# First head's scores before the last query tile, the last value block's cast on ScalarE, and a new order of transposes, in a cross-attention and expert kernel

## The reference

```
x = x + xattn(layernorm(x), ctx)     # 16 heads of 32 columns
x = x + ffn(layernorm(x))            # 8 experts, gated by a narrow zone of a sigmoid

xattn:  q = (x @ Wq + bq) / sqrt(32);  k, v = split(ctx @ Wkv + bkv)
        q, k rounded to 127 steps per row and head; v to 127 steps per column
        attn = softmax(q k^T) per head, rounded to 255 steps per row
        out  = (attn @ v) @ Wp + bp
ffn:    weights = gate(sigmoid(x @ Wr / temperature))
        out = sum_e weights_e * (silu(x @ Wg_e) * (x @ Wu_e)) @ Wd_e
```

## Time and profile before

| | |
|---|---|
| median of 3 runs | 743.71 us (742.88, 743.71, 746.09) |
| profiled execution | 742.73 us, of which the span of the trace is 740.9 us |
| TensorE busy | 623.8 us, 84% |
| VectorE busy | 573.1 us, 77% |
| ScalarE busy | 461.5 us, 62% |
| GpSimd busy | 371.5 us, 50% |
| DMA queue of SP | 114.48 MB, 71.5% of 16 engines |
| span of attention on VectorE | 133.08 to 445.5 us |

### The profile page before, as it was taken

The page is one execution under the profiler, slowest core; times in us unless marked ns, Lnnn a source line. Parts: engine busy times, 40 slices in busy tenths (PEclk is TensorE's granted clock), DMA queues, the critical chain, the costliest instruction groups (busy, mean ns, idle before and its releaser), DMA issues. The chain is left out here.

```text
span 740.9 us, 15739 instructions
## 1 busy us (share of the span) xinstructions
PE 623.8 (84%) x5298; PEld 325.9 (44%) x5298; DVE 573.1 (77%) x974; ACT 461.5 (62%) x552; POOL 371.5 (50%) x394
## 2 busy tenths in 40 slices
PE   6999999566777777777767687799999999999993
PEld 2444443233434343343434355455555555555551
DVE  4997778999999999999999996784746537455330
ACT  6334358688899999999999997243434435344321
POOL 5254457544666675757576754215334453343503
PEclk9999999999999999999999999899999999999997
DMA  7767767999999999999999995459895887977804
GB/s 246 195 150 168 167 142 124 189 170 179 181 171 191 211 174 213 174 217 181 206 180 210 188 201 107 133 178 183 223 250 127 235 220 184 254 137 213 149 6 57
DMA packets 325908, 131.25 MB, mean 177 GB/s; under 512 B 300901, under 2 KB 300901, under 8 KB 325865
## 3 DMA queue, kind: packets, MB, share of 16 engines
q1 hardware_dynamic: 318688, 114.48, 71.5%
q0 software_dynamic: 7168, 16.26, 10.6%
q10 hardware_dynamic: 8, 0.01, 0.0%
HBM read 44.33 MB, written 12.06 MB: 76 GB/s over the span
## 5 line engine op out<-in xcount | busy, mean ns | idle before, releaser
L946 ACT ACTIVATE work<-spare,exp_bias 128x2048 int16<-128x2048 f32 (+1 forms) x128 | 255.5, 1996 | 32.0 <-DVE exp_bias L1276 30.4
L1267 DVE TENSOR_SCALAR_CACHE_REDUCE spare<-psum,q_step_now 128x1024 f32<-128x1024 f32 x128 | 162.2, 1274 | 0.1
L632 POOL CAST work<-work 128x2048 int16<-128x2048 uint8 x63 | 119.1, 1890 | 81.8 <-DMA work<-work 67.5
L1258 DVE TENSOR_SCALAR_CACHE_REDUCE spare<-psum,q_step_now 128x2048 f32<-128x2048 f32 x64 | 150.4, 2350 | 0.1
L1679 PE MATMUL psum<-keys_region,work 128*128 128x512 f16 x256 | 73.1, 383 | 52.1 <-DVE spare L1267 28.9
L1679 PE MATMUL psum<-keys_region,bias_hl 128*128 128x512 f16 x256 | 71.9, 382 | 32.1 <-DVE spare L1267 28.3
L737 POOL DMA_INDIRECT work<-x_rows,slot_tok x32 | 50.1, 1564 | 97.1 <-DVE slot_w L1453 73.8
L749 POOL DMA_INDIRECT out_dram<-keys_region,slot_tok x32 | 51.7, 1617 | 74.1 <-ACT keys_region L1025 67.1
L1521 PE MATMUL psum<-work,spare 128*128 128x480 f16 (+1 forms) x396 | 79.2, 360 | 0.9 <-DVE work L1426 0.9
L1521 PE MATMUL psum<-work,keys_region 128*128 128x480 f16 x384 | 78.9, 366 | 0.0
L1639 PEld LDWEIGHTS psum<-values_region,work 128*128 128x128 f16 x2048 | 67.4, 96 | 24.2 <-DMA work<-work 12.5
(11 more groups left out here) (222 smaller groups left out, 1014.0 us busy)
## 6 DMA issues: line engine op xcount, KB each, us to landing
spare<-in_L_ffn_Wd_dram SPq DMA_DIRECT2D x8, 1024.0 KB, 15.6
spare<-in_L_ffn_Wg_dram SPq DMA_DIRECT2D x7, 1024.0 KB, 5.7
spare<-in_L_ffn_Wu_dram SPq DMA_DIRECT2D x7, 1024.0 KB, 12.1
work<-in_ctx_dram SPq DMA_DIRECT2D x3, 1024.0 KB, 5.7
work<-work SPq DMA_TRANSPOSE x181, 3.6
token_region<-in_L_xattn_Wkv_dram SPq DMA_DIRECT2D x2, 1024.0 KB, 6.9
resid<-in_x_dram SPq DMA_DIRECT2D x2, 1024.0 KB, 8.7
x_rows<-work SPq DMA_DIRECT2D x8, 256.0 KB, 2.3
```

The costliest lines, as they stand in the source:

```text
L632: nc.gpsimd.tensor_copy(p_T_int[h % 4 // 2], pair_bytes[h % 4 // 2]).then_inc(unpacked, 1)
L946: nc.scalar.activation(last_int[h % 2] if words and h >= H - 2 else p_int[h % 4], scores, ACT.Exp, bias=exp_bias[:, h % 4:h % 4 + 1], scal ...
L1258: nc.vector.tensor_scalar(staged[h % 4], psum[:, at:at + 4, :].rearrange("p b k -> p (b k)"), q_step_now[:, h:h + 1], None, ALU.mult, ALU.min,
L1267: nc.vector.tensor_scalar(staged[h % 4][:, 1024 * c:1024 * c + 1024], psum[:, at:at + 2, :].rearrange("p b k -> p (b k)"), q_step_now[:, h ...
```

## The change

It has five parts.

1. TensorE makes the scores of head 0 of the first tile after query tile 6, and query tile 7 after them. VectorE stages head 0 and gives its bias first, and takes query tile 7 then.
2. The cast of the last value block goes from VectorE to ScalarE, behind `cut_queries(2)`. `cut_queries(3)` goes behind the first exponential.
3. The steps in `q_step_now` come from ScalarE for the first tile as well, straight from `q_quantum` with the factor in the instruction; the tensor `q_step` is gone, and so are VectorE's two instructions for steps.
4. On SP the transpose of the last value block goes from before p_0 to before p_1, and the two of the last pair of query tiles from before p_0 to behind p_3 and p_4. `vT_in` becomes two semaphores.
5. GpSimd waits for all transposed queries behind its first three unpacks and not ahead of clearing the second half of `q_now`.

```diff
@@ SP
-            for i in range(2):
-                transpose_values(2 * i)
-                transpose_values(2 * i + 1)
-                transpose_queries(i + 2)
-            sp.wait_ge(vT_in, 16 * DK)
+            transpose_values(0)
+            transpose_values(1)
+            transpose_queries(2)
+            transpose_values(2)
...
                     sp.wait_ge(exp_done, u + 1)
                     passed()
+                    if first and h == 1:
+                        transpose_values(DK - 1)
+                    if first and h % 2 and h < 4:
+                        sp.wait_ge(vT_in[h // 2], 32)
...
+                    if first and h in (3, 4):
+                        transpose_queries(DK - 1, range(h - 3, h - 2))
@@ POOL
-            for b in range(2):
-                pool.wait_ge(qT_in[b], 16 * QT // 2)
             pool.wait_ge(q_full, QT)
             pool.wait_ge(wp_ready, DK)
             clear_queries(own, 1)
             queries_now(0, 1)
             norm_base = own.base + own.n
+            pool.wait_ge(vT_in[0], 32)
             unpack(0, 0, True)
+            pool.wait_ge(vT_in[1], 32)
             unpack(0, 2, True)
             unpack(0, 4)
             pool.wait_ge(unpacked, 3)
+            for b in range(2):
+                pool.wait_ge(qT_in[b], 16 * QT // 2)
             next_queries(1, 0)
@@ ACT
             cut_queries(2)
-            cut_queries(3)
+            act.wait_ge(v_rounded, DK)
+            nc.scalar.activation(v_T_int[:, DK - 1, :], v_i16[:, DK - 1, :], ACT.Copy).then_inc(last_halved, 1)
...
-                nc.scalar.activation(q_step_now[:, these], q_step[:, bass.ds(i, 1), these].rearrange("p a h -> p (a h)"), ACT.Copy
-                                     ).then_inc(steps_ready, 1)
+                nc.scalar.activation(q_step_now[:, these], q_quantum[:, bass.ds(i, 1), these].rearrange("p a h -> p (a h)"), ACT.Copy,
+                                     scale=-1.0 / WS).then_inc(steps_ready, 1)
...
+            for n in range(2):
+                copy_steps(0, n)
+
             def attention_tile(i, first, after_rows, following=True):
                 for h in range(H):
                     u = H * i + h
+                    if first and h == 1:
+                        cut_queries(DK - 1)
@@ DVE
             query_tiles(2, 4, 2)
-            halve_values(3)
             query_tiles(3, 6, 1)
-            nc.vector.tensor_scalar(q_step_now[:, :], q_quantum[:, 0, :], -1.0 / WS, None, ALU.mult).then_inc(first_steps, 1)
-            query_tiles(4, 7, 1)
-            own = Steps(dve, dve_step, head + query_steps * (DK + 1))
-            own.link(nc.vector.tensor_scalar(q_step[:, :, :], q_quantum[:, :, :], -1.0 / WS, None, ALU.mult))
...
                     stage_whole(i, h, first)
-                    if h:
+                    if first and h == 0:
+                        make_bias(i, h)
+                        query_tiles(DK, QT - 1, 1)
+                    elif h:
                         make_bias(i, h - 1)
...
-            dve.wait_ge(first_steps, 1)
+            dve.wait_ge(steps_ready, 2)
@@ PE
-            for t in range(QT):
+            def queries(t):
...
+            for t in range(QT - 1):
+                queries(t)
...
                 if first and h == 1 and n == 0:
-                    pe.wait_ge(q_out, DK + 1)
+                    pe.wait_ge(q_out, DK)
...
                 for n in range(2):
                     scores(i, 0, n, first)
+                if first:
+                    queries(QT - 1)
                 for h in range(0, H, 2):
                     scores(i, h + 1, 0, first)
+                    if first and h == 6:
+                        pe.wait_ge(q_out, DK + 1)
```

## The result

| | before | changed |
|---|---|---|
| median of 20 runs | 743.36 us (741.91 to 746.09) | 744.89 us (743.03 to 747.71) |
| ratio of the runs | | 1.0022, 95% interval 1.0012 to 1.0031 |
| profiled execution, its span | 742.73, 740.9 | 745.16, 743.4 |

The changed kernel is slower by 1.53 us in the medians and by 0.22% in the ratio. The forecast was +0.35 us, no change that a measurement can tell; 0.22% is inside 0.5% and inside the stated range, but the interval excludes 1, and the size is more than four times the forecast.

What follows compares the result with a forecast made beforehand. The prediction took VectorE to bound attention, with the DMA engines near their limit: -0.95 us at the start and +1.3 of stalls make +0.35, so 743.71 becomes 744.1 us, with 742.0 to 746.4 for 8 in 10.

Steps and rivals of the forecast that it cites:

- The bound and the gap: Attention: VectorE, busy 239.89 of 240 us, sets the time; behind p_0 the DMA engines stand idle some 5 us.
- The start: Start of attention: VectorE 0.95 us earlier from head 1 on.
- The 3.16 us: VectorE's start: the cast of the last value block 1.53, first steps 0.64 and all steps 0.99 us go.
- The new wait for ScalarE: Behind query tile 6, VectorE waits for head 0's steps from ScalarE, 127.88 to 129.85: 2.0 us.
- The stalls: From head 1 on, transposes displaced among the probabilities land late and cost VectorE 1.3 us.
- p_1, forecast 1.4 late and 0.1: Transpose p_1 lands at 148.6 where TensorE wants it at 147.2: 1.4 us late, costs 0.1.
- p_3, forecast 0.4 late and no cost: Transpose p_3, issued at 148.1, lands at 152.55: 0.4 us late, which costs nothing.
- the server with fixed times: SP's transposes, served in order: 1.85 us from issue, then 1.35 for 8 blocks or 2.6 for 16.
- the cover of 1.3: Values on TensorE: a probability transpose can be 1.3 us late before VectorE has to wait.
- p_5, forecast 2.2 late and 0.9: Transpose p_5 lands at 159.2 where 156.9 is wanted: 2.2 us late, 0.1 already lost, costs 0.9.
- p_7, forecast 0.3: Transpose p_7, behind a load of weights, lands at 164.4 where 162.8 is wanted: costs 0.3 us.
- The rival in which the queue doesn't recover: From p_5 on SP's queue stays full and p_7 to p_13 miss too: up to +4.4 us, 748.1; chance 0.12.

Runs made afterwards that it cites:

- e5: The kernel before, run again without an edit: attention 320.78 us against 320.68, ratio 0.9993.
- e1: Changed kernel with the last value block's transpose moved ahead of p_0 and the last query pair's directly behind p_0: attention 319.86 us, ratio to the kernel before 1.0002.
- e4: Kernel before with only the new order of SP's transposes and GpSimd's waits: attention 322.23 us, ratio to the kernel before 1.0036.
- e9: The changed kernel again, without further edits: attention 323.24 us, ratio to the kernel before 1.0030.
- e10: e1 again, without further edits: attention 320.20 us, ratio to the kernel before 0.9992.
- e2: Changed kernel with only the last value block's transpose moved ahead of p_0: attention 321.19 us, ratio to the kernel before 1.0017.
- e3: Changed kernel with only the last query pair's two transposes moved to behind p_0: attention 321.97 us, ratio to the kernel before 1.0007.
- e8: Changed kernel with six more throwaway matmuls ahead of the values in four slots of the first tile: attention 322.99 us, ratio to the kernel before 1.0036.
- e11: e7 again, without further edits: attention 319.26 us, ratio to the kernel before 0.9966.
- e6: Changed kernel with ScalarE's two copies of steps ahead of its cut of query tiles 4 and 5: attention 321.54 us, ratio to the kernel before 1.0003.
- e7: Changed kernel with the edits of both e1 and e6: attention 319.84 us, ratio to the kernel before 0.9969.

## Why the prediction was right in its main mechanism and short in size

**The number.** 744.1 against 744.89 looks closer than it was. The 743.71 that it started from was the median of three runs; of twenty it is 743.36, so that the difference, +0.35 against +1.53, is the fair comparison. The prediction also named a sign of being wrong in the main, a shift of attention by more than 1.5 us. From the mark the shift was 1.90 us (1.07 in the times of the two profiles as they stand, which don't start alike), so by this sign the prediction was wrong. So the main mechanism held, the sizes did not, and the lower clock was missing; the terms below say where.

**The bound and the gap: right.** VectorE had no idle before (0.56 us at 199 us in e5), and every idle that came is in the time. SP's gap behind p_0, the late p_1, p_3 and p_5, and TensorE's waits at values(1) and values(5) came as described.

**The start, forecast -0.95: too large.** It was -0.65 in the first pair of profiles. The prediction had the first staging 5.01 us behind the mark (129.85 - 124.84), then 2.53 for head 0 with its bias, then 2.04 for query tile 7. Measured were 4.93, 2.47 and 2.47, which makes 9.87. So the step that failed is that tile 7 costs the same wherever it stands: its small instruction at 132.12 took 0.60 us, where it took 0.17 in the kernel before and in e1. In e1 tile 7 took 2.04, and head 1 came at 9.38.

The gain at the start is in any case hardly larger than its scatter. The old order had head 1 at 10.52, 10.18 (e5) and 9.86 (e4), mean 10.19; the order of the change at 9.38 to 10.28 in seven profiles (changed, e9, e1, e10, e2, e3, e8), mean 9.77. That is 0.4 us on average, and -0.04 in the pair of e9 and e5.

A part of this scatter is in small instructions that wait for GpSimd. The 3.16 us read off as removed work held such waits too. The first steps ran 129.41 to 130.14 before, 0.73 us for 16 columns; a subtraction on GpSimd ended at 130.10. In e5 the ends were 129.04 and 129.00, and all steps ended 0.09 behind the next subtraction, at 131.86 and 131.77. In e4 the first steps took 0.38. In e11 the same kind of small instruction ran 1.14, and GpSimd's subtraction beside it ended with it:

```profile
130.39 1.14 DVE L1195 TENSOR_SCALAR scratch<-row_scales 128x16 f32<-128x16 f32 x1
```

```profile
130.34 1.15 POOL L684 TENSOR_TENSOR work<-spare,work 128x512 f16<-128x512 f32 x1
```

131.53 and 131.49. In the changed kernel's timeline of VectorE, at 125.41 and 132.12, 1.10 and 0.60 us stand at the two places, where 0.17 was the time of the same instruction in tile 7 of e5. The first ended at 126.51, a subtraction at 126.48. The second ended at 132.72 with no subtraction beside it (GpSimd had begun a multiplication at 132.01), and what held it isn't shown. So a hold can go on to the next small instruction when its bearer is removed, and isn't saved then. It depends on how the streams fall against each other: in e2 and e8 both instructions took 0.17 to 0.19. (The first hold in the changed kernel lay under the wait for ScalarE; the second did not.)

**The new wait for ScalarE, forecast 2.0: right.** It was 1.31 behind a tile that was itself 0.93 late, 2.2 together, and 2.01 in e1.

**The stalls, forecast 1.3: they were 1.83, and 1.82 in e9.** In the changed kernel, by terms:

- p_1, forecast 1.4 late and 0.1: TensorE waited 1.29, VectorE lost nothing.
- p_3, forecast 0.4 late and no cost: TensorE waited 1.24, since p_3 took 5.5 us to land where the server with fixed times, from v_3's issue at 141.19, has 4.7; the windows show 82 GB/s between 150 and 152 us at a share of 1.35. That lateness was inside the cover of 1.3. It cost 0.88 all the same, because the clock was at 0.50 behind it and the scores took longer. Here a step failed: the cover was worked out from rows at full clock, and the prediction gave the clock no term. e8 showed it, by giving the clock back at this place (p_3's values began 0.26 us earlier there too, less than the 0.88); in e2 and e3 too, idle came with the clock at 0.50 around waits of 1.20 to 1.27. A wait doesn't always bring it: behind the 1.29 us for p_1 the clock stayed at 1.00. e8 also showed that the 0.88 doesn't add to the sum, since p_5 would have taken it.
- p_5, forecast 2.2 late and 0.9: TensorE waited 1.80, VectorE lost 0.41 + 0.54 = 0.95. That the sum agrees is luck. The landing was forecast 34.4 us behind the mark (159.2 - 124.84) and came after 35.3 (159.29 - 124.01): 0.4 of this because v_3 was issued later, and 0.5 because the transposes from v_3 on took longer than the server has them. That was the larger step that failed. It should have cost more, but 0.88 had been lost at p_3 already. The second piece, 0.54, isn't the lateness as forecast; it came with the clock at 0.50, from 161 to 164 us. In e9 the clock was at 1.00 there: TensorE waited 1.55, and VectorE lost 0.21.
- p_7, forecast 0.3: TensorE waited 0.63, VectorE lost nothing.

**Sum.** From head 1 on VectorE took 2.55 us longer. Its stagings start 0.42, 0.63, 0.49 and 0.63 us later at the four idles, 2.17 in all for 1.83 of idle: without a wait a staging starts up to 0.07 us before the end of the one before, and with one it doesn't. At 201 us it is 0.30 more, which is not the change's (e5 lost 0.45 there), and 0.08 are in small differences. With -0.65 this makes the 1.90 measured. The forecast of -0.95 + 1.3 had both terms wrong in the same direction, by 0.3 and 0.9. Seen from p_5, the first staging behind it was forecast level with the kernel before and came 0.99 later (37.10 us behind the mark against 36.11), nearly all of it the later landing; 0.63 more came with the clock behind it, and 0.30 at 201 us.

**The rule of the Trainium skill** ("DMA: Bandwidth & Descriptors", "Latency and other measured facts", 261 GB/s for a DMA transpose) gave -0.95 in all. The windows of the changed kernel show 209 and 215 GB/s in the stretches from 144 to 148 us in which the queue held nothing but transposes. Only behind the window of 82 GB/s is there one of 273, and the two together make 178. p_5 was late: the measurement decides against the rule here.

**The rival in which the queue doesn't recover** did not come: p_7 was in time for VectorE, and from 170 us on one idle of 0.39 is left. In e9 p_7 cost 0.28 + 0.54 with the clock at 0.50, and p_9, 0.30 late, cost nothing.

## What to carry to other kernels

A queue that is taken up to 0.99 has no room for moved work behind its gap: 32 blocks of 5.4 us cost VectorE 2.2 to 2.5 us from head 1 on in the wrong place, in four pairs of profiles, and next to nothing in the gap a few entries ahead (310.48 and 310.81 us against 310.16 and 310.60 before). Ask of each moved transfer where the queue stands empty, not only whether it is wanted late. And work out the cover of a late transfer at the lower clock too, for an engine that waits for it may come back at half speed: here 1.3 us of cover became 0.7. Of several late transfers the last that exceeds its cover sets the time, and a gain at an earlier one is lost there.

## What the runs showed of the hardware that was not expected

- TensorE's granted clock was 0.50 behind waits of 1.24 and 1.80 us in the changed kernel (from 154 to 157 and from 161 to 164 us); in the kernel before, with waits of 0.8 us at most in that stretch, it stayed at 1.00. At 0.50 eight matmuls of 128x512 took 3.50 us. The length of one wait doesn't decide it: the clock stayed at 1.00 behind the wait of 1.29 us for p_1 in the changed kernel, and behind this one in the kernel before, while e5, the same kernel, was at 0.50 from 131 to 134 us behind a wait of 2.56.

```profile
132.12 0.60 PE L1679 MATMUL psum<-keys_region,work 128*128 128x512 f16 x2 [2.90 <-DVE work L1188]
```

- A VectorE instruction of 16 columns that began 0.04 to 0.09 us behind a tensor_tensor on GpSimd (1.15 us, from two tensors in SBUF) ended 0.02 to 0.04 us behind its end: 0.17 us became 1.10 to 1.15 in four profiles (changed, e6, e7, e11). In e9 the same instruction began 0.09 us ahead of the subtraction and took 0.17.
- A DMA transpose of 16 blocks landed after 4.6, 5.0 and 5.5 us in the same queue. Every profile has stretches of 2 us between 144 and 182 us in which the engines were busy (share 1.2 to 1.7) but moved only 57 to 147 GB/s.
